# First cross attention of a decoder: weights divided before they are turned, exponentials head by head

## The chip, the cores and the metric

One core of a Trainium2 chip runs the kernel. The metric is device time in microseconds (us) of one execution; the profile is of one execution, taken by the hardware profiler. Engines: PE is TensorE, DVE VectorE, ACT ScalarE, POOL GpSimd, SP SyncE.

## The reference

Two decoder layers, on x of 8 x 256 x 256 and a context of 8 x 120 x 256, f32. Layer 0 is self attention (16 heads of 64), cross attention to the context (16 heads of 16), and a feed-forward stage with rounded weights; layer 1 is a gated attention, a second cross attention and a coupled feed-forward net. A layer norm follows each. What the change touches is the first cross attention:

```
q = split_heads(query @ Wq.T + bq)
k = split_heads(key @ Wk.T + bk)
v = split_heads(value @ Wv.T + bv)
scores = jnp.einsum('bhnd,bhmd->bhnm', q, k)
attn = jax.nn.softmax(scores, axis=-1)
out = jnp.einsum('bhnm,bhmd->bhnd', attn, v)
out = out.transpose(0, 2, 1, 3).reshape(B, N, D_MODEL)
return out @ Wo.T + bo
```

## The kernel before

**Passes.** Four passes (NI), each over two batches (NB), 512 rows in tiles of 128 (T = 4, TS = 2 per batch). one_pass(it, last, then) runs attn0, cross0, ffn0, attn1, cross1 and coupled_ffn. Each engine has its program written out by hand, in an order that never changes, and waits on semaphores (a Signal counts per pass). To fill TensorE, projections of the next pass stand in the stages of this one: values0(then, n), queries0 and keys0. In the last pass `then` is None and spin(n) issues dummy matmuls in some places.

**cross0, a unit.** The work of the first cross attention is cut into UX = 8 units n, in the order batch b = n // 4, half c of the 16 heads = n // 2 % 2, row tile st = n % 2. A unit has HC = 8 heads against M = 120 context columns: 960 score columns on 128 rows. M is 120, S (rows of a batch) 256, P 128, DH 16.

**TensorE.** turn_normed turns the normed x1 of a batch; queries_x(b) projects it; scores_x(n) (matmuls at L757) writes 2 x 480 columns into the pair of banks SCORE_X[n % 2]; turn_x(n) (L770, 16 transposes) turns ex into banks 4 and 5, [120, 1024]; weigh_x(m) (L789), m for batch and half of the heads, takes two units: the first kind of matmuls multiplies by the values vxp, the second by pair_ones and so makes each head's sum, beside it in the same bank; out_x(b) (L525) projects with Wo. scores_x(n) waits until unit n - 2 has been subtracted (dx_done), turn_x(n) for the exponential (px_done) and for the copy of unit n - 1.

**VectorE.** max_x(n): a maximum per row and head (L1954), and, behind a wait for it and for the turning of unit n - 2, the subtraction into ex (L1959), which has two buffers. divide_x(m): a reciprocal of the sums (L1968) and a product into oxt (L1970). sum_2(b) adds the residual (L1928) and calls norm_summed (statistics, L1748 to L1761; GpSimd's power at L2344; apply_norm, L1767). quantize(b) prepares the feed-forward stage, whose first product on VectorE is L1991.

```
for n in range(UX):
    max_x(n)
    if n in (4, 6):
        divide_x(n // 2 - 2)
divide_x(2)
sum_2(0)
divide_x(3)
apply_norm(it, "2", of(res), xs["2"], 0)
quantize(0)
sum_2(1)
```

**ScalarE.** keep (L1341), keep_queries (L1352) and keep_v0 (L1358) copy projections out of PSUM; exp_x(n) is one exponential of 128x960 in place (L1440); keep_tx(n) copies the turned unit into ext (L1446); load_table (L1399) changes the function table.

**GpSimd.** mask_x(m) (L2370) spreads the keys of a half over eight masked copies, kxm, which scores_x(2m) needs; the reciprocal square roots (L2344) stand behind. Elsewhere in its program: scaling of the self attention's weights (L2358), residual plus bias (L2381), a norm with two scalars (L2393).

The self attention of layer 0 already has the form that the change gives to cross0 (exp0 with bias and accumulator at L1388, inverse0 at L1828, L2358 on GpSimd), and so has the exponential of the second cross attention in part (L1614, with bias and accumulator from PSUM, 120x256).

## Time and profile before

| | |
|---|---|
| median of 3 runs | 1120.45 us (1120.40 to 1120.66) |
| profiled execution, its own time | 1121.52 us |
| span of the profiled execution | 1119.8 us |
| mean granted TensorE clock | 0.994 of full speed |
| TensorE, VectorE, ScalarE, GpSimd busy | 92%, 71%, 57%, 28% |
| instructions | 19639 |

The span runs from the first to the last instruction; the execution's own time has what lies around it, 1.7 us. Times in rows are from the start of the span. The second pass's cross0 begins near 377 us and ends near 420, the last pass's near 910 and 950. A busy TensorE is not TensorE at its peak, since ends of matmuls are modelled. "idle before" is the time that an engine waited in front of a row, with what ended the wait.

### The profile page before, as it was taken

What the parts mean: (1) busy time and instruction counts of PE and PEld (TensorE: products, weight loads), DVE (VectorE), ACT (ScalarE), POOL (GpSimd) and SP (SyncE); (2) the same over time, 40 slices, a digit from 0 to 9 for tenths busy, and PEclk for the clock granted to TensorE, in tenths of its full rate; (3) what the DMA queues carried; (4) which work ended last, traced back from release to release, by engine and by line L of the source; (5) the groups of instructions that cost most, each with busy time, mean ns of one, the idle gap of its engine ahead of it and who ended that gap; (6) DMA issues with size and microseconds to landing.
All of it is one profiled execution on the core that took longest, in us unless ns stands there. A gap on an engine that the chain in (4) does not pass through costs nothing.

```text
span 1119.8 us, 19639 instructions
## 1 busy us (share of the span) xinstructions
PE 1031.2 (92%) x7176; PEld 676.7 (60%) x7184; DVE 798.6 (71%) x1880; ACT 635.3 (57%) x1728; POOL 310.3 (28%) x666
## 2 busy tenths in 40 slices
PE   8999999998899999999889999999889998898886
PEld 4477557854557655775547755775455665576463
DVE  3584886668697488658778588666869758864777
ACT  2573556376477257459468365647647724644833
POOL 1264202240056301142108420224004630224110
PEclk9999999999999999999999999999999999999999
DMA  9250000000010000000000000000000000000000
GB/s 345 60 173 1 20 3 7 1 1 1 1 39 1 20 2 9 1 1 1 1 19 21 1 20 1 11 1 1 1 1 20 2 1 1 1 1 1 2 1 20
DMA packets 15951, 22.77 MB, mean 20 GB/s; under 512 B 2160, under 2 KB 13424, under 8 KB 15728
## 3 DMA queue, kind: packets, MB, share of 16 engines
q1 hardware_dynamic: 15408, 21.50, 5.9%
q8 instruction: 58, 0.95, 0.4%
q14 instruction: 37, 0.30, 0.1%
q10 hardware_dynamic: 448, 0.02, 0.0%
HBM read 19.42 MB, written 2.10 MB: 19 GB/s over the span
## 4 chain that ended last, share of the span: by engine, by line
PE 51%; DVE 26%; ACT 12%; issue 6%; POOL 2%; DMA 2%; SPq 0%; DVEq 0%; POOLq 0%; ACTq 0%
PE PS L525 8%; PE PS L929 4%; PE PS L694 4%; ACT work L1388 4%; PE PS L680 3%; PE PS L643 3%; ACT work L1614 3%; PE PS L556 3%; PE PS L898 2%; DVE stat L1748 2%; PE PS L660 2%; PE PS L789 2%; DVE maxx L1954 2%; PE PS L500 2%; DVE work L1959 2%
## 5 line engine op out<-in xcount | busy, mean ns | idle before, releaser
L2344 POOL TENSOR_TENSOR rstd<-var,minus_half 128x2 f32<-128x2 f32 x64 | 45.8, 715 | 529.5 <-DVE var L1761 529.5
L1614 ACT ACTIVATE work<-PS,nmax 120x256 f32<-120x256 f32 x256 | 118.3, 485 | 18.4 <-DVE nmax L2185 17.8
L2185 DVE TENSOR_REDUCE nmax<-PS 120x2 f32<-120x512 f32 x128 | 82.4, 686 | 35.9 <-PE PS L929 35.5
L1821 DVE TENSOR_REDUCE nmax<-PS 128x2 f32<-128x512 f32 x128 | 82.3, 679 | 13.0 <-PE PS L643 13.0
L1388 ACT ACTIVATE work<-PS,nmax 128x256 f32<-128x256 f32 x176 | 81.5, 486 | 15.1 <-DVE nmax L1821 14.9
L2358 POOL TENSOR_SCALAR work<-work,inv 128x256 f32<-128x256 f32 x176 | 81.1, 479 | 0.0
L2339 POOL TENSOR_TENSOR pool_pause<-minus_half 128x1 f32<-128x1 f32 x96 | 28.5, 297 | 182.4 <-DVE inv L1828 94.0
L643 PE MATMUL PS<-work 64*128 64x256 f32 x512 | 70.0, 397 | 6.6 <-ACT work L1388 5.6
L1341 ACT COPY turned_a<-PS 128x512 f32<-128x512 f32 x24 | 14.1, 589 | 100.9 <-PE PS L500 100.9
L643 PEld LDWEIGHTS PS<-work 64*128 64x128 f32 x512 | 44.8, 186 | 27.4 <-ACT work L1388 14.6
L694 PE MATMUL PS<-wo,work 128*128 128x256 f32 x256 | 58.5, 384 | 0.0
L1767 DVE TENSOR_SCALAR x_room<-res,mv,rstd 128x256 f32<-128x256 f32 x96 | 36.0, 416 | 30.2 <-POOL rstd L2344 30.2
L1614 ACT ACTIVATION_READ_ACCUMULATOR work<-PS,nmax 120x1 f32 x256 | 55.6, 217 | 0.0
L694 PEld LDWEIGHTS PS<-wo,work 128*128 128x128 f32 x256 | 47.6, 190 | 8.1 <-issue 1.5
L573 PE MATMUL PS<-turned_x,wk 128*128 128x512 f32 x96 | 50.4, 622 | 0.0
L1440 ACT ACTIVATE work<-work 128x960 f32<-128x960 f32 x32 | 32.1, 1003 | 31.3 <-DVE work L1959 31.3
L1748 DVE BATCH_NORM_STATS2 stat<-res 128x6 f32<-128x256 f32 x128 | 48.1, 418 | 2.0
L556 PE MATMUL PS<-turned_x,wq 128*128 128x512 f32 x96 | 46.4, 596 | 0.0
L525 PE MATMUL PS<-late,turned_a 128*128 128x256 f32 x192 | 46.3, 387 | 0.0
L544 PE MATMUL PS<-wv,turned_x 128*128 128x512 f32 x96 | 46.1, 602 | 0.0
L1954 DVE TENSOR_REDUCE maxx<-PS 128x8 f32<-128x960 f32 x32 | 36.8, 1149 | 12.4 <-PE PS L757 12.4
L680 PE MATMUL PS<-work 128*64 128x256 f32 x352 | 44.4, 385 | 0.0
(275 smaller groups left out, 2535.2 us busy)
## 6 DMA issues: line engine op xcount, KB each, us to landing
turned_x<-in_x_turned_dram SPq DMA_DIRECT2D x4, 512.0 KB, 3.6
xa<-in_x_dram SPq DMA_DIRECT2D x4, 512.0 KB, 4.3
out_dram<-x_room SPq DMA_DIRECT2D x4, 512.0 KB, 3.0
rows<-in_rows_dram SPq DMA_DIRECT2D x1, 1536.0 KB, 10.8
late<-in_L_attn_W_dram SPq DMA_DIRECT2D x2, 768.0 KB, 8.1
wv<-in_attn_v_dram SPq DMA_DIRECT2D x2, 512.0 KB, 5.8
wq<-in_attn_q_dram SPq DMA_DIRECT2D x1, 1024.0 KB, 8.9
wk<-in_attn_k_dram SPq DMA_DIRECT2D x1, 1024.0 KB, 10.9
```

What stands on the lines that cost most here:

```text
L525: mm = pe.matmul(bank(n)[:, (t % 2) * width:(t % 2 + 1) * width], lhs[:, k, t * P:(t + 1) * P], weight[:, k, :], start=(k == 0), stop=(k = ...
L556: mm = pe.matmul(bank(7), wq0[:, k, j * P:(j + 1) * P], turned_x[:, k, :], start=(k == 0), stop=(k == KD - 1))
L643: mm = pe.matmul(bank(2 * (u % 2) + hh)[:, st * S:(st + 1) * S], q0[rows, j, b * S + st * P:b * S + (st + 1) * P], k0[rows, j, b, :], star ...
L680: mm = pe.matmul(bank(6)[hh * DH0:(hh + 1) * DH0, b * S:(b + 1) * S], v0[:, TS * b + tt, (2 * j + hh) * DH0:(2 * j + hh + 1) * DH0], e0t[u ...
L694: mm = pe.matmul(bank(t // 2)[:, (t % 2) * D:(t % 2 + 1) * D], o0t[:, j, t * P:(t + 1) * P], wo0[:, j, :], start=(j == 0), stop=(j == J - 1))
L1388: op = act.activation(e0[u % 3][:, st, hh, :], bank(2 * (u % 2) + hh)[:, st * S:(st + 1) * S], ACT.Exp, bias=nmax0[:, u % 2, hh, st:st + 1 ...
L1614: op = act.activation(e1[:, par, r, kv, :], bank(SCORE_1[r])[0:M, kv * S:(kv + 1) * S], ACT.Exp, bias=nmax1[:, par, r, kv:kv + 1], accum_o ...
L1748: op = dve.bn_stats(stat[:, t, :], src(t))
L1821: dve.tensor_reduce(nmax0[:, u % 2, hh, :], bank(2 * (u % 2) + hh).rearrange("p (t s) -> p t s", t=TS), AX.X, ALU.max, negate=True).then_i ...
L1954: dve.tensor_reduce(maxx[:, n % 2, :].rearrange("p (g h) -> p g h", g=2), banks, AX.X, ALU.max).then_inc(mx_done.sem, 1)
L2185: dve.tensor_reduce(nmax1[:, par, r, :], bank(SCORE_1[r])[0:M, :].rearrange("p (v s) -> p v s", v=2), AX.X, ALU.max, negate=True).then_inc ...
L2358: op = pool.tensor_scalar(e0[u % 3][:, st, hh, :], e0[u % 3][:, st, hh, :], inv0[:, u % 2, hh, st:st + 1], 1.0, ALU.mult, ALU.mult)
```

## The change

- The maximum is written negated (nmaxx). exp_x(n) reads the scores in PSUM, head by head: eight exponentials of 128x120, each with its bias and with its sum over the head's columns (sumx). The subtraction goes.
- inverse_x(n) on VectorE takes the reciprocal of the eight sums; divide_x(n) on GpSimd multiplies the whole unit by it, in place, [128, 8, 120] with the reciprocal broadcast along the 120 columns. turn_x(n) now waits for that (nx_done). ex has three buffers.
- weigh_x has the values' matmuls alone; divide_x(m) on VectorE becomes a copy on ScalarE, keep_ox(m). pair_ones goes.
- keep_tx is on VectorE for units 0, 1, 3, 4, 6 and 7, and stays on ScalarE for 2 and 5.
- The orders of TensorE, ScalarE, VectorE and GpSimd in cross0 are written anew: scores run two units ahead of the turnings, queries_x(0) stands before values0(then, 0), the values of the next pass stand elsewhere, out_x(0) stands before the last two turnings, add_2 and norm_summed are apart; spin(2) in the last pass goes.

The diff, with lines of context left out (eight columns of indent too):

```diff
-pair_ones = sb("pair_ones", [P, 2, 2 * DH])
...
-ex = view(work, K + 1024, P, [2, HC, M])
-maxx = sb("maxx", [P, 2, HC])
+ex = [view(work, K + 1024, P, [HC, M]), view(work, K + 1024 + HC * M, P, [HC, M]), view(work, Q, P, [HC, M])]
+nmaxx, sumx, invx = (sb(n, [P, 2, HC]) for n in ("nmaxx", "sumx", "invx"))
...
-invx = view(work, R + 1440, P, [S])
...
-sx_done, mx_done, dx_done, px_done = (signal(n, UX) for n in ("sx_done", "mx_done", "dx_done", "px_done"))
+sx_done, mx_done, px_done, ix_done, nx_done = (
+    signal(n, UX) for n in ("sx_done", "mx_done", "px_done", "ix_done", "nx_done"))
...
-avx_done, ix_done, ox_kept = (signal(n, NB * KD) for n in ("avx_done", "ix_done", "ox_kept"))
+avx_done, ox_kept = (signal(n, NB * KD) for n in ("avx_done", "ox_kept"))
...
-N_CONST = 12
+N_CONST = 10
...
-            pe.wait_ge(dx_done.sem, dx_done.at(it, n - 1))
+            pe.wait_ge(px_done.sem, px_done.at(it, n - 1))
...
     def turn_x(it, n):
-        pe.wait_ge(px_done.sem, px_done.at(it, n + 1))
+        pe.wait_ge(nx_done.sem, nx_done.at(it, n + 1))
...
-                mm = pe.transpose(bank(4 + half)[0:M, h * 64:(h + 1) * 64], ex[rows, n % 2, h, :], ident[rows, rows])
+                mm = pe.transpose(bank(4 + half)[0:M, h * 64:(h + 1) * 64], ex[n % 3][rows, h, :], ident[rows, rows])
...
-            pe.wait_ge(dx_done.sem, dx_done.at(it, UX))
-        for kind in range(2):
-            for par in range(2):
-                for r in range(4):
-                    lhs = (vxp[:, b, 4 * c + r, par:par + 2, :] if kind == 0 else pair_ones[0:M, par, :])
-                    mm = pe.matmul(bank(WEIGH_X[m])[32 * r:32 * r + 32, kind * S:(kind + 1) * S], lhs,
-                                   ext[:, m % 2, 2 * r + par, :], start=(par == 0), stop=(par == 1))
+            pe.wait_ge(px_done.sem, px_done.at(it, UX))
+        for par in range(2):
+            for r in range(4):
+                mm = pe.matmul(bank(WEIGH_X[m])[32 * r:32 * r + 32, 0:S], vxp[:, b, 4 * c + r, par:par + 2, :],
+                               ext[:, m % 2, 2 * r + par, :], start=(par == 0), stop=(par == 1))
...
     def out_x(it, b):
...
-        pe.wait_ge(dx_done.sem, dx_done.at(it, UX - 1))
+        pe.wait_ge(px_done.sem, px_done.at(it, UX - 1))
...
     def cross0(it, then=None):
         turn_normed(it, "x1", xs["1"], 0)
-        if then is not None:
-            values0(then, 0)
         queries_x(it, 0)
         turn_normed(it, "x1", xs["1"], 1)
...
-            values0(then, 1)
+            values0(then, 0)
         scores_x(it, 0)
         scores_x(it, 1)
         queries_x(it, 1)
         scores_x(it, 2)
+        if then is not None:
+            values0(then, 1)
         turn_x(it, 0)
         scores_x(it, 3)
+        scores_x(it, 4)
         turn_x(it, 1)
-        scores_x(it, 4)
+        if then is not None:
+            values0(then, 2)
+        scores_x(it, 5)
         turn_x(it, 2)
+        scores_x(it, 6)
+        turn_x(it, 3)
         weigh_x(it, 0, then)
-        scores_x(it, 5)
-        turn_x(it, 3)
-        if then is not None:
-            values0(then, 2)
-        scores_x(it, 6)
+        scores_x(it, 7)
         turn_x(it, 4)
+        if then is not None:
+            values0(then, 3)
         weigh_x(it, 1)
-        scores_x(it, 7)
         turn_x(it, 5)
-        if then is not None:
-            values0(then, 3)
+        out_x(it, 0)
         turn_x(it, 6)
+        if then is not None:
+            values0(then, 4)
+        turn_x(it, 7)
         weigh_x(it, 2)
-        turn_x(it, 7)
-        out_x(it, 0)
         weigh_x(it, 3)
-        if then is not None:
-            values0(then, 4)
-        else:
-            spin(2)
         out_x(it, 1)
...
             values0(then, 5)
...
     def cross0(it, then=None):
         def exp_x(n):
-            act.wait_ge(dx_done.sem, dx_done.at(it, n + 1))
-            act.activation(ex[:, n % 2, :, :], ex[:, n % 2, :, :], ACT.Exp).then_inc(px_done.sem, 1)
+            act.wait_ge(mx_done.sem, mx_done.at(it, n + 1))
+            if n > 2:
+                act.wait_ge(tx_done.sem, tx_done.at(it, 2 * n - 4))
+            for h in range(HC):
+                op = act.activation(ex[n % 3][:, h, :], bank(SCORE_X[n % 2] + h // 4)[:, h % 4 * M:(h % 4 + 1) * M], ACT.Exp,
+                                    bias=nmaxx[:, n % 2, h:h + 1], accum_out=sumx[:, n % 2, h:h + 1])
+            op.then_inc(px_done.sem, 1)
...
         def keep_tx(n):
...
+        def keep_ox(m):
+            b, c = m // KD, m % KD
+            act.wait_ge(avx_done.sem, avx_done.at(it, m + 1))
+            act.copy(oxt[:, c, b * S:(b + 1) * S], bank(WEIGH_X[m])[:, 0:S]).then_inc(ox_kept.sem, 1)
+
         keep(it, "x1", 0)
+        keep(it, "x1", 1)
+        keep_queries(it, 0, 4, qx, col["L0_xattn_bq"], qx_done, qx_kept)
...
             keep_v0(then, 0)
-        keep_queries(it, 0, 4, qx, col["L0_xattn_bq"], qx_done, qx_kept)
-        keep(it, "x1", 1)
+        exp_x(0)
+        exp_x(1)
+        keep_queries(it, 1, 5, qx, col["L0_xattn_bq"], qx_done, qx_kept)
+        exp_x(2)
...
             keep_v0(then, 1)
-        exp_x(0)
-        keep_queries(it, 1, 5, qx, col["L0_xattn_bq"], qx_done, qx_kept)
-        exp_x(1)
-        keep_tx(0)
-        exp_x(2)
-        keep_tx(1)
         exp_x(3)
+        exp_x(4)
         keep_tx(2)
-        exp_x(4)
-        keep_tx(3)
+        exp_x(5)
...
             keep_v0(then, 2)
-        exp_x(5)
-        keep_tx(4)
+        keep_ox(0)
         exp_x(6)
+        exp_x(7)
+        keep_ox(1)
+        if then is not None:
+            keep_v0(then, 3)
         keep_tx(5)
-        exp_x(7)
-        keep_tx(6)
-        if then is not None:
-            keep_v0(then, 3)
-        keep_tx(7)
+        keep_ox(2)
+        keep_ox(3)
...
             keep_v0(then, 4)
...
         apply_norm(it, "1", of(res), xs["1"], 1)
...
-        def sum_2(b):
+        def add_2(b):
...
-            norm_summed(it, "2", b)
...
         def max_x(n):
...
-            dve.tensor_reduce(maxx[:, n % 2, :].rearrange("p (g h) -> p g h", g=2), banks, AX.X, ALU.max
+            dve.tensor_reduce(nmaxx[:, n % 2, :].rearrange("p (g h) -> p g h", g=2), banks, AX.X, ALU.max, negate=True
...
-            dve.wait_ge(mx_done.sem, mx_done.at(it, n + 1))
+
+        def inverse_x(n):
+            dve.wait_ge(px_done.sem, px_done.at(it, n + 1))
...
-                dve.wait_ge(tx_done.sem, tx_done.at(it, 2 * n - 2))
-            dve.tensor_tensor(ex[:, n % 2, :, :].rearrange("p (g h) m -> p g h m", g=2), banks,
-                              maxx[:, n % 2, :].rearrange("p (g h o) -> p g h o", g=2, o=1).to_broadcast([P, 2, 4, M]),
-                              ALU.subtract).then_inc(dx_done.sem, 1)
-
-        def divide_x(m):
-            b, c = m // KD, m % KD
-            dve.wait_ge(avx_done.sem, avx_done.at(it, m + 1))
-            if m > 0:
-                dve.wait_ge(ox_kept.sem, ox_kept.at(it, m))
-            dve.reciprocal(invx[:, :], bank(WEIGH_X[m])[:, S:2 * S]).then_inc(ix_done.sem, 1)
-            dve.wait_ge(ix_done.sem, ix_done.at(it, m + 1))
-            dve.tensor_tensor(oxt[:, c, b * S:(b + 1) * S], bank(WEIGH_X[m])[:, 0:S], invx[:, :], ALU.mult
-                              ).then_inc(ox_kept.sem, 1)
-
-        for n in range(UX):
-            max_x(n)
-            if n in (4, 6):
-                divide_x(n // 2 - 2)
-        divide_x(2)
-        sum_2(0)
-        divide_x(3)
+                dve.wait_ge(nx_done.sem, nx_done.at(it, n - 1))
+            dve.reciprocal(invx[:, n % 2, :], sumx[:, n % 2, :]).then_inc(ix_done.sem, 1)
+
+        def keep_tx(n):
+            dve.wait_ge(tx_done.sem, tx_done.at(it, 2 * n + 2))
+            if n > 3:
+                dve.wait_ge(avx_done.sem, avx_done.at(it, n // 2 - 1))
+            dve.tensor_copy(ext[:, n // 2 % 2, :, n % 2 * P:(n % 2 + 1) * P].rearrange("p h (f i) -> p f h i", f=2),
+                            PS[0:M, 4:6, :].rearrange("p f (h i) -> p f h i", i=64)).then_inc(tx_kept.sem, 1)
+
+        max_x(0)
+        max_x(1)
+        inverse_x(0)
+        max_x(2)
+        inverse_x(1)
+        keep_tx(0)
+        max_x(3)
+        inverse_x(2)
+        max_x(4)
+        keep_tx(1)
+        inverse_x(3)
+        max_x(5)
+        inverse_x(4)
+        max_x(6)
+        keep_tx(3)
+        inverse_x(5)
+        max_x(7)
+        inverse_x(6)
+        keep_tx(4)
+        inverse_x(7)
+        add_2(0)
+        keep_tx(6)
+        norm_summed(it, "2", 0)
+        keep_tx(7)
         apply_norm(it, "2", of(res), xs["2"], 0)
         quantize(0)
-        sum_2(1)
+        add_2(1)
+        norm_summed(it, "2", 1)
         apply_norm(it, "2", of(res), xs["2"], 1)
         quantize(1)
...
+        def divide_x(n):
+            pool.wait_ge(ix_done.sem, ix_done.at(it, n + 1))
+            pool.tensor_tensor(ex[n % 3][:, :, :], ex[n % 3][:, :, :],
+                               invx[:, n % 2, :].unsqueeze(2).to_broadcast([P, HC, M]), ALU.mult).then_inc(nx_done.sem, 1)
+
         mask_x(2)
+        divide_x(0)
+        divide_x(1)
         mask_x(3)
+        for n in range(2, UX):
+            divide_x(n)
         rstds_of(it, "2")
...
-    pool.memset(pair_ones[:, :, :], 0.0).then_inc(filled.sem, 1)
-    pool.wait_ge(filled.sem, 7)
-    pool.memset(pair_ones[:, 0, 0:DH], 1.0).then_inc(const_ready.sem, 1)
-    pool.memset(pair_ones[:, 1, DH:2 * DH], 1.0).then_inc(const_ready.sem, 1)
+    pool.wait_ge(filled.sem, 6)
...
-    pool.wait_ge(filled.sem, 9)
+    pool.wait_ge(filled.sem, 8)
...
```

## Rows read from the trace of the kernel before

**Rows 1.** The page: busy time of the engines, and the chain of waits by engine

```profile
PE 1031.2 (92%) x7176; PEld 676.7 (60%) x7184; DVE 798.6 (71%) x1880; ACT 635.3 (57%) x1728; POOL 310.3 (28%) x666
...
PE 51%; DVE 26%; ACT 12%; issue 6%; POOL 2%; DMA 2%; SPq 0%; DVEq 0%; POOLq 0%; ACTq 0%
```

**Rows 2.** Chain of waits, second pass: start us, us, what

```profile
419.45 0.70 DVE res L1928
...
425.44 1.29 DVE work L1991
```

**Rows 3.** Timeline of PE, second pass: start us, us, engine, line, operation [idle before]

```profile
394.29 1.07 PE L789 MATMUL PS<-work,vxp 120*32 120x256 f32 x16
395.18 1.05 PE L789 MATMUL PS<-work,pair_ones 120*32 120x256 f32 x16
...
416.38 1.99 PE L525 MATMUL PS<-x0TWo,work 128*128 128x256 f32 x8 [0.43 <-DVE work L1970]
```

**Rows 4.** Timeline of DVE, second pass

```profile
384.72 1.16 DVE L1954 TENSOR_REDUCE maxx<-PS 128x8 f32<-128x960 f32 x1 [3.54 <-PE PS L757]
385.91 1.16 DVE L1959 TENSOR_TENSOR work<-PS,maxx 128x960 f32<-128x960 f32 x1
...
403.02 1.76 DVE L1968 RECIPROCAL work<-PS 128x256 f32<-128x256 f32 x1
404.81 0.42 DVE L1970 TENSOR_TENSOR work<-PS,work 128x256 f32<-128x256 f32 x1
```

**Rows 5.** Groups by form on DVE, whole span: busy us, mean ns, idle before

```profile
L1828 DVE RECIPROCAL inv<-sum 128x4 f32<-128x4 f32 x64 | 11.2, 175 | 19.3 <-ACT work L1388 15.5 <-ACT x_room L1388 1.9
```

**Rows 6.** Timeline of ACT, second pass

```profile
388.01 0.82 ACT L1352 ACTIVATE work<-PS,cols 128x256 f32<-128x256 f32 x2
389.36 1.00 ACT L1440 ACTIVATE work<-work 128x960 f32<-128x960 f32 x1 [0.53 <-DVE work L1959]
390.27 0.99 ACT L1446 COPY work<-PS 120x1024 f32<-120x1024 f32 x1
```

**Rows 7.** Timeline of ACT in the second cross attention, first pass

```profile
258.26 0.47 ACT L1614 ACTIVATE work<-PS,nmax 120x256 f32<-120x256 f32 x1
258.63 0.19 ACT L1614 ACTIVATION_READ_ACCUMULATOR work<-PS,nmax 120x1 f32 x1
...
259.62 0.48 ACT L1614 ACTIVATE work<-PS,nmax 120x256 f32<-120x256 f32 x1
```

**Rows 8.** Groups by form on ACT, whole span

```profile
L1589 ACT ACTIVATE xh_room<-PS,cols 128x256 f32<-128x256 f32 x48 | 20.1, 470 | 19.2 <-PE PS L898 19.2
...
L1673 ACT ACTIVATE work<-PS,g_b 64x128 f32<-64x128 f32 x8 | 2.8, 356 | 5.8 <-PE PS L1006 5.8
```

**Rows 9.** Groups by form on POOL, whole span

```profile
L2358 POOL TENSOR_SCALAR work<-work,inv 128x256 f32<-128x256 f32 x176 | 81.1, 479 | 0.0
...
L2393 POOL TENSOR_SCALAR x_room<-res,mv,rstd_h 128x256 f32<-128x256 f32 x16 | 20.5, 1284 | 0.9
L2381 POOL TENSOR_TENSOR x_room<-x_room,rows 128x1024 f32<-128x1024 f32 x4 | 9.4, 2352 | 3.4 <-DVE x_room L1767 3.4
```

**Rows 10.** Stretches: length, busy us by engine, then granted PE clock, DMA, GB/s

```profile
383.60:418.30 34.70, 31.39 (x326) 17.50 (x326) 30.24 (x39) 20.02 (x24) 3.82 (x12) 1.00 0.03 10
418.30:445.87 27.57, 26.92 (x143) 15.26 (x143) 23.75 (x62) 19.26 (x25) 2.53 (x3) 1.00 0.03 10
...
264.00:268.00 4.00, 2.67 (x32) 1.41 (x32) 3.59 (x9) 3.81 (x13) 0.00 (x0) 1.00 0.00 0
```

**Rows 11.** The same for two stretches of the last pass

```profile
934.00:936.00 2.00, 0.43 (x13) 0.32 (x10) 1.97 (x3) 1.73 (x2) 0.00 (x0) 0.96 0.00 0
936.00:938.00 2.00, 2.00 (x28) 1.37 (x32) 1.97 (x2) 0.00 (x0) 0.00 (x0) 0.50 0.00 0
```

**Rows 12.** Timeline of DVE, last pass

```profile
915.50 1.16 DVE L1954 TENSOR_REDUCE maxx<-PS 128x8 f32<-128x960 f32 x1 [1.76 <-PE PS L757]
...
950.14 0.68 DVE L1928 TENSOR_TENSOR res<-PS,x_room 128x512 f32<-128x512 f32 x1
```

More of the change, by code:

```diff
@@ L1152, in cross0 @@
                 scores_x(it, 2)
+                if then is not None:
+                    values0(then, 1)
                 turn_x(it, 0)
                 scores_x(it, 3)
+                scores_x(it, 4)
                 turn_x(it, 1)
-                scores_x(it, 4)
-                turn_x(it, 2)
-                weigh_x(it, 0, then)
-                scores_x(it, 5)
-                turn_x(it, 3)
                 if then is not None:
                     values0(then, 2)
+                scores_x(it, 5)
+                turn_x(it, 2)
                 scores_x(it, 6)
+                turn_x(it, 3)
+                weigh_x(it, 0, then)
+                scores_x(it, 7)
                 turn_x(it, 4)
-                weigh_x(it, 1)
-                scores_x(it, 7)
-                turn_x(it, 5)
                 if then is not None:
                     values0(then, 3)
+                weigh_x(it, 1)
+                turn_x(it, 5)
+                out_x(it, 0)
                 turn_x(it, 6)
-                weigh_x(it, 2)
-                turn_x(it, 7)
-                out_x(it, 0)
-                weigh_x(it, 3)
                 if then is not None:
                     values0(then, 4)
-                else:
-                    spin(2)
+                turn_x(it, 7)
+                weigh_x(it, 2)
+                weigh_x(it, 3)
                 out_x(it, 1)
```

2 lines of the change are left out of this document (1 added, 1 removed).

## The prediction

> **What bounds the kernel now.** I read four views in this order. The page [rows 1] says that TensorE is busy 92% of the span and carries half of the chain of waits, VectorE a quarter. That is an average; the change touches one stage, so the rest is read there. The stage runs once in each of the four passes; the second pass (turning of x1 from about 377.5 us) stands for the first three, the last pass has no work of a next pass in it.
>
> The chain of waits [rows 2] runs over VectorE at the stage's end: the sum of the second batch at 419.45, then with no other engine but one short GpSimd step the first gate product at 425.44. The timelines say why. VectorE works almost without a gap from 384.72: a maximum (1.15) and a subtraction (1.16) for each of eight units, and four times a reciprocal (1.76) and a product (0.42) [rows 4]. ScalarE is slack: one exponential of 960 columns takes 1.00 [rows 6], and from 383.60 to 418.30 it is busy 20.02 us of 34.70. TensorE is busy 31.39 us of that stretch, and behind the stage, from 418.30 to 445.87, it is busy 26.92 of 27.57 [rows 10]. So behind the stage TensorE and VectorE run nearly level: what makes out_x(1) late makes everything late, with 0.65 us of TensorE's gaps as the only cushion.
>
> **The change part by part.** *VectorE* loses eight subtractions (9.3 us) and four reciprocals with products (8.7 us) and gains six copies of turned weights (960 columns take 1.16 [rows 4], so 1024 some 1.22 and six 7.3 us) and eight small reciprocals (175 ns each [rows 5]). It becomes slack until exp_x(7). *TensorE* loses the row sums: in each of four weigh_x the pair_ones half, of the length of the first half, which starts 0.89 before it (394.29, 395.18 [rows 3]); with the hand-over 3.7 us per pass. The score, turn and projection matmuls stay. *Set-up* loses three memsets of GpSimd at the very start, while TensorE waits for its first weights: nothing. The two dummy matmuls of the last pass go as well: no cost by themselves. No transfer is added, removed or moved.
>
> *GpSimd* gets one product of 128x960 per unit. The trace does not show it. Nearest is the in-place product-shaped TENSOR_TENSOR of 128x1024 with a broadcast operand, 2.35 us, so 2.2; the dearest form per column is L2393, 1284 ns for 256, which would make 4.8; the cheapest, the scaling by a scalar (479 for 256), 1.8 [rows 9]. I take 2.2, as the operation is the same and the size nearly so; that its broadcast runs along the inner index, and not the outer, no row prices. Queued behind these products on GpSimd is mask_x(3), which scores_x(6) needs five microseconds later: hidden. Who waits for the product is turn_x, with everything behind it in TensorE's fixed order.
>
> *ScalarE* is where the bill comes. An exponential of 960 columns starts the next instruction 0.91 after its own start (389.36 to 390.27 [rows 6]). It becomes eight of 120 columns, each with an accumulator read. The heads' price: L1614, an exponential from PSUM with bias and accumulator, starts every 0.453 us at 256 columns (258.26 to 259.62 is three) [rows 7]. An activation of 128 columns is 114 ns shorter than one of 256, 356 against 470 [rows 8], 0.89 ns per column; a plain pair of 256 (0.82 for two, less the 0.09 that an instruction overlaps the next, so 0.37 each) against the 0.91 for 960 gives 0.77 [rows 6]. For 136 columns fewer that is 0.105 to 0.121. A head costs **0.337**, a unit 2.70 instead of 0.91. Bounds: 0.45 if nothing is saved with width; 0.26 if the read (0.08, from 0.453 against the plain 0.37) were free. 0.337 is a reading between rows that differ only in width, so I hold 0.325 to 0.35 for near certain unless the read behaves otherwise.
>
> The Trainium skill ("ScalarE: Activation LUTs", section "What ACT_TABLE_LOAD costs") gives an ACTIVATE with a pointer bias about 280 ns + 0.833 per column, less 93 of overlap; an estimate by it alone is 0.287 a head, and the sum below would come to between -1 and -2 us instead of +10. It prices no accumulator read; at 256 columns it gives 0.400, and this trace shows 0.453.
>
> Now the walk, second pass. The first maximum ends at 385.88 as before [rows 4] (the values that moved behind the queries fill the same time). From there ScalarE's queue never waits: each scores_x(n) waits for exp_x(n-2), and 0.1 + 0.9 (matmuls) + 1.15 (maximum) = 2.2 us fit under the 2.70 of exp_x(n-1), as does inverse 0.2 + product 2.2 + turning 0.6 = 3.0 under two exponentials, the three buffers allowing that. In the queue stand eight units, 21.6, keep_queries(1) 0.75, two value copies 1.0, one keep_tx 0.92, one keep_ox 0.35: 24.6 us. exp_x(7) ends at **410.5**. Behind it: keep_ox(1) 0.35, hand-over 0.15, out_x(0) 1.9 (413.0), turning 6 0.6, values 1.9 (415.5), turning 7 0.6 (416.1). VectorE meanwhile does add_2(0) 0.7, keep_tx(6) 1.2, the statistics 1.3 (416.2), only then keep_tx(7), which sits in front of the last weighing: 417.4. Then weigh 3 1.0, keep_ox(3) 0.4, hand-overs 0.3, out_x(1) 1.9: it ends at **420.9**, against 418.3 (416.38 and 1.9 [rows 3]): +2.6 us. The 3.7 us that TensorE is spared become gaps, since it waits for exponentials and then for keep_tx(7) and keep_ox(3).
>
> VectorE's side: the second sum starts at 421.0 instead of 419.45 [rows 2], +1.5. TensorE's side: its work up to the end of the feed-forward stage is unchanged, with 0.65 us of gaps [rows 10], which a shift can use up in part: +2.6 less 0.3 = +2.3. The larger one counts: **+2.3** in each of the first three passes. Nothing later in a pass gives it back, because both engines are full up to 445.87.
>
> The last pass: the copy of queries_x(0) now stands behind the copy of the second turning on ScalarE, and scores_x(0) waits for it with no values as cover, so the first maximum starts 1.5 us later than at 915.50 [rows 12] and the first exponential at 918.1. The queue is 1.0 shorter without the value copies, but waits 0.5 in sum for maxima: exp_x(7) ends at 942.2, and with the same tail of 10.4 out_x(1) ends at 952.6. The second sum, at 950.14 before [rows 12], starts at 952.7: **+2.5**. There the granted clock stands at 0.50 from 936 to 938, its lower level of 1.2 GHz, behind 2 us with TensorE 0.43 us busy [rows 11]. With TensorE waiting for exponentials about half the time this comes again, likely more than once, and the tail has 6 us of TensorE work in the chain; a slice of 2 us at half rate adds 1. I add **+1**.
>
> Sum: 3 x 2.3 + 2.5 + 1 = +10.4. The profiled execution took 1121.52 for a span of 1119.8; the median of the runs is 1120.45, 0.1% less. Against the median the change gives 1130.9, rounded **1130.5**. A run can tell about 0.2% (2.2 us) from no change.
>
> **Rivals.**
> 1. *The accumulator read half hides behind the next head.* A head then costs 0.30, midway between 0.337 and the lower bound of 0.26. Every 0.01 us is 64 heads x 0.01 = 0.64 a pass, so 0.037 less takes the 2.3 a pass to 0: 1120 to 1122, within 0.2%. For it: the read's record overlaps its neighbours. Against: the start distance of 0.453 has that overlap in it already [rows 7]. 12%. The estimate of 0.287 by the Trainium skill ("ScalarE: Activation LUTs") lies on this side of the forecast; by it the time would be about 1119.
> 2. *The other side: faster.* The same place, ScalarE's queue of 64 heads; it decides at 0.30 a head, below which the 18 us of VectorE and 3.7 us of TensorE begin to pay. With the read wholly free, 0.26, the queue is 4.9 us shorter than forecast; TensorE's order then binds and passes on some 4.3 of it, -2.0 a pass: 1113. 14%.
> 3. *GpSimd becomes the bound*: above 3.1 us a product the eight in a row outlast the exponentials, at 3.4 the pass gains 4.5 (1139), at 4.8 16 us (1184). For it: the L2393 form; against: the 1024 product [rows 9]. 7%.
> 4. *The clock falls in the first three passes too.* Around 391.6 to 395.0 TensorE would be busy some 45%. One slice at half rate per pass costs about 1.3: 1134 to 1137. Against: 264 to 268 has TensorE busy 2.67 of 4 us and keeps 1.00 [rows 10]. 12%.
> The forecast itself, head 0.325 to 0.35 and no more: 55%, 1126 to 1134.
>
> **How the numbers follow.** The point is the forecast's. The range from 1118.5 to 1137 holds the forecast, rivals 1 and 4; it leaves out rival 3 and the fast part of rival 2, together under 0.2. Slower: 0.55 + 0.07 + 0.12 = 0.74; within 0.2%: 0.12; faster 0.14.
>
> **What would show it.** Right: 256 activations of 128x120 (eight heads, eight units, four passes), starting every 0.34; ScalarE without a gap from the first maximum to the eighth unit, the eighth ending 24.6 us after the first starts; maxima waiting for scores; the product on GpSimd near 2.2; TensorE's idle before keep_tx and keep_ox; the second sum 1.5 us later within the pass. Wrong: a head under 0.30 or over 0.37, a GpSimd product over 3.1, ScalarE waiting for maxima, or a slow clock in the middle passes.

## The result, and where the time went

The changed kernel takes **1137.38 us** (median of 4 runs, 1135.72 to 1145.51), the kernel before beside it 1120.49: a ratio of 1.0162, with an interval of 1.0142 to 1.0183. That is +16.9 us where I had forecast +10, and 0.4 us above my range. Two more measurements of the same kernel (both in experiment 2) gave ratios of 1.0119 and 1.0136.

The profiled execution took 1136.96 us for a span of 1134.5, 14.7 more than the span of before. The page of the kernel after, its busy times and its chain by engine, against [rows 1]:

```profile
PE 1024.7 (90%) x6916; PEld 673.3 (59%) x6924; DVE 763.1 (67%) x1872; ACT 673.7 (59%) x2200; POOL 368.7 (32%) x695
...
PE 51%; ACT 19%; DVE 19%; issue 6%; POOL 3%; DMA 2%; SPq 0%; DVEq 0%; POOLq 0%; ACTq 0%
...
L1438 ACT ACTIVATE work<-PS,nmaxx 128x120 f32<-128x120 f32 x256 | 89.9, 471 | 9.2 <-DVE nmaxx L1956 9.2
...
L2402 POOL TENSOR_TENSOR work<-work,invx 128x960 f32<-128x960 f32 x32 | 57.3, 1791 | 37.0 <-DVE invx L1963 37.0
```

VectorE's busy time fell by 35 us and ScalarE's share of the chain rose from 12% to 19%. (The 471 ns of an exponential is the length of its record, which overlaps its neighbours; the start distance is what counts.) GpSimd's product takes 1.79 us.

Where in the program the time goes is read by setting the same event of both traces side by side. I take two: VectorE's first sum of a pass (ahead of the first cross attention) and its second output sum (behind it). Timeline of VectorE of the kernel before, second and last pass:

```profile
373.42 0.69 DVE L1916 TENSOR_TENSOR res<-PS,xa 128x512 f32<-128x512 f32 x1 [6.47 <-PE PS L694]
...
905.97 0.69 DVE L1916 TENSOR_TENSOR res<-PS,xa 128x512 f32<-128x512 f32 x1 [6.47 <-PE PS L694]
```

The second sums of before stand in [rows 2] (419.45) and [rows 12] (950.14). The same of the kernel after:

```profile
374.62 0.69 DVE L1919 TENSOR_TENSOR res<-PS,xa 128x512 f32<-128x512 f32 x1 [6.47 <-PE PS L693]
...
422.50 0.69 DVE L1931 TENSOR_TENSOR res<-PS,x_room 128x512 f32<-128x512 f32 x1 [0.44 <-PE PS L524]
...
912.49 0.69 DVE L1919 TENSOR_TENSOR res<-PS,xa 128x512 f32<-128x512 f32 x1 [6.47 <-PE PS L693]
...
966.30 0.69 DVE L1931 TENSOR_TENSOR res<-PS,x_room 128x512 f32<-128x512 f32 x1 [3.41 <-PE PS L524]
```

I call the distance from the one to the other **the stage**. Before it is 46.03 us in the second pass (and in the first and third) and 44.17 in the last; after it is 47.88 (+1.85) and **53.81 (+9.64)**. Some 23 us later the feed-forward stage adds 0.37 in each of the first three passes, which makes 2.22 a pass. Between the stages the two traces drift apart or together by up to 1.6 us (+0.54 ahead of the first stage, -1.57 from the first pass to the second, +0.76 to the last, -1.43 behind it). Three of these four go with short stretches at a granted clock near 0.7, at 285 to 295 us and at 1055 to 1060 before, and at 810 to 815 after. Every trace of this study has such stretches outside the last stage, at changing places, and I treat what they cost as noise.

So three passes behave alike and the last does not. Timeline of TensorE in the last pass of the kernel after, and its windows (length, busy us of PE, PEld, DVE, ACT, POOL, granted clock, DMA share, GB/s):

```profile
922.38 3.55 PE L756 MATMUL PS<-work 64*128 64x480 f32 x8 [1.42 <-ACT work L1347]
...
951.05 3.78 PE L524 MATMUL PS<-x0TWo,work 128*128 128x256 f32 x8 [0.60 <-ACT work L1452]
954.76 1.11 PE L769 MATMUL PS<-ident,work 64*120 64x64 f32 x16
957.31 1.11 PE L769 MATMUL PS<-ident,work 64*120 64x64 f32 x16 [1.44 <-DVE work L1969]
958.35 3.64 PE L786 MATMUL PS<-work,vxp 120*32 120x256 f32 x32
962.48 3.78 PE L524 MATMUL PS<-x0TWo,work 128*128 128x256 f32 x8 [0.49 <-ACT work L1452]
```

```profile
383.60:418.30 34.70, 28.05 (x243) 14.43 (x241) 18.72 (x29) 28.15 (x141) 19.37 (x20) 1.00 0.05 17
...
946.00:950.00 4.00, 2.19 (x47) 1.49 (x45) 2.46 (x3) 4.00 (x27) 2.77 (x2) 0.96 0.00 0
950.00:954.00 4.00, 3.40 (x16) 2.67 (x13) 0.20 (x1) 1.91 (x7) 1.88 (x2) 0.50 0.00 0
954.00:958.00 4.00, 2.56 (x31) 1.74 (x32) 2.71 (x7) 0.00 (x0) 0.00 (x0) 0.50 0.00 0
958.00:962.00 4.00, 3.99 (x40) 1.55 (x37) 3.68 (x13) 0.37 (x1) 0.71 (x1) 0.50 0.02 4
962.00:966.00 4.00, 3.52 (x8) 2.86 (x9) 0.85 (x3) 1.86 (x3) 0.00 (x0) 0.50 0.00 0
```

Both out_x take 3.78 us where [rows 3] has 1.99: from 950 to 966 TensorE is granted 0.50, its level of 1.2 GHz, and in this stretch the chain of waits runs over TensorE (from 951.05 to 966.28 it names another engine for 1.6 us alone). The clock was low earlier in this stage too, for shorter stretches: the scores of units 0 and 1 take 3.55 us at 922.38, where two in a row take 1.88 in the second pass. In the second pass (first row) the same stage keeps 1.00.

### The profile page after: what moved, and what is told of

Its sections match the earlier page's. It is cut to its first block, busy times and chain, and to the rows that moved or that the text cites. A ratio compares the mean times of both kernels' runs of the same rounds, so it can differ in the third digit from the quotient of the medians.

```text
span 1134.5 us, 19620 instructions
## 1 busy us (share of the span) xinstructions
PE 1024.7 (90%) x6916; PEld 673.3 (59%) x6924; DVE 763.1 (67%) x1872; ACT 673.7 (59%) x2200; POOL 368.7 (32%) x695
## 4 chain that ended last, share of the span: by engine, by line
PE 51%; ACT 19%; DVE 19%; issue 6%; POOL 3%; DMA 2%; SPq 0%; DVEq 0%; POOLq 0%; ACTq 0%
PE PS L524 9%; ACT work L1438 7%; PE PS L926 4%; ACT work L1383 3%; PE PS L679 3%; PE PS L642 3%; PE PS L693 3%; PE PS L555 3%; PE PS L895 2%; ACT work L1617 2%; PE PS L543 2%; DVE stat L1751 2%; PE PS L659 2%; POOL rstd L2361 2%; PE PS L499 2%
## 5 line engine op out<-in xcount | busy, mean ns | idle before, releaser
L1438 ACT ACTIVATE work<-PS,nmaxx 128x120 f32<-128x120 f32 x256 | 89.9, 471 | 9.2 <-DVE nmaxx L1956 9.2
L1438 ACT ACTIVATION_READ_ACCUMULATOR work<-PS,nmaxx 128x1 f32 x256 | 74.9, 317 | 0.0
L2402 POOL TENSOR_TENSOR work<-work,invx 128x960 f32<-128x960 f32 x32 | 57.3, 1791 | 37.0 <-DVE invx L1963 37.0
L642 PEld LDWEIGHTS PS<-work 64*128 64x128 f32 x512 | 44.7, 186 | 27.5 <-ACT work L1383 14.7
L1956 DVE TENSOR_REDUCE nmaxx<-PS 128x8 f32<-128x960 f32 x32 | 36.7, 1156 | 34.6 <-PE PS L756 34.6
L756 PE MATMUL PS<-work 64*128 64x480 f32 x128 | 36.4, 653 | 21.2 <-ACT work L1438 19.8
## 6 DMA issues: line engine op xcount, KB each, us to landing
rows<-in_rows_dram SPq DMA_DIRECT2D x1, 1536.0 KB, 10.8
```

The lines of the kernel that those rows point to most:

```text
L642: mm = pe.matmul(bank(2 * (u % 2) + hh)[:, st * S:(st + 1) * S], q0[rows, j, b * S + st * P:b * S + (st + 1) * P], k0[rows, j, b, :], star ...
L1438: op = act.activation(ex[n % 3][:, h, :], bank(SCORE_X[n % 2] + h // 4)[:, h % 4 * M:(h % 4 + 1) * M], ACT.Exp, bias=nmaxx[:, n % 2, h:h + ...
```

## The experiments

My theory after the result: **ScalarE's queue costs 2.2 to 2.5 us a pass as forecast, and TensorE's half clock in the last pass costs 7 more.** Rivals: the two dropped dummy matmuls did it; GpSimd's product did it; the loss comes with the gaps and not with the clock; the place of the low clock is chance.

**1. The dropped dummies alone, and dummies in all gaps.** a0_spin2 puts back what the change dropped:

```diff
                 weigh_x(it, 3)
+                if then is None:
+                    spin(2)
                 out_x(it, 1)
```

a1_spins has such lines at thirteen places, 56 dummies in the last pass (its text on record says 61, that of a5_light_spins 60; both are miscounts), three of which the changed kernel has as well, behind out_x(1): behind the second turning 5, queries 1: 3, scores 2: 9, scores 3: 4, turn_x 1: 6, and so on. b1_before_spins gives the kernel before six, ahead of turn_x(5).

> The changed kernel with the two dummy matmuls put back before the last out_x of the last pass, which the change dropped with its else branch. Main theory (TensorE runs at 1.2 GHz in the last pass because its short instructions lie apart for some 25 us in that stretch, long before these dummies): two dummies behind the last weigh_x come too late, so the last pass keeps its loss of 9.7 us and the time stays within 1 us of the changed kernel, about 1137. Rival (the dropped dummies alone let the clock fall): the last pass loses 2.5 us instead of 9.7, about 1130.

> The changed kernel with 61 dummy matmuls in the gaps of TensorE in the last pass's cross0, beside the same work. Main theory (7.2 us of the last pass's loss of 9.7 are TensorE at half clock, 2.5 us are the queue of ScalarE as in the other passes): the granted clock stays 1.00 from 910 to 970 us, the two last weigh_x and out_x take 1.99 us or less instead of 3.6 to 3.8, and the time falls by 6 to 8 us, to about 1130. Rival (the low clock only follows from a stretch that waits for ScalarE, and costs little by itself): the clock is back, the time falls by 2 us or less, to 1135 or more.

> The kernel before with six dummy matmuls ahead of turn_x(5) in the last pass, where its own granted clock stood at 0.66. Main theory: the low clock of the kernel before is short and lies where TensorE waits for others, so it was worth 1 us at most: 1119.5 to 1120.5. Rival: it was worth 2 us or more, so the last pass of the kernel before is no clean reference, and the loss by the clock in the changed kernel is larger than 7.2 us.

Measured (kernel before beside them 1121.02): a0 1135.3, ratio 1.013 [1.0109, 1.015]; its last stage takes 48.87 us in the one trace, at a clock of 0.58 to 0.87 in four of the 5-us windows from 935 to 960, and a further stretch at 0.5 to 0.8 lies at 825 to 840. The stage loses 4.7 us here and not the 9.7 that I expected; the stretch at 825 to 840 lies outside it, and the distance from the third stage to the last is 225.45 us against 221.39 in the kernel after. The low clock stays, so the dropped dummies are not its cause; whether they soften it the runs do not say, since a0's ratio lies between those of the unaltered change. b1 1121.14, ratio 1.0002 [0.9992, 1.0011], stage 44.26: its six dummies lift the clock from 935 to 940 from 0.66 to 1.00, and no time comes back. So the kernel before loses nothing there and is a clean reference.

a1 is a miss: 1140.0, ratio 1.0176. The clock is 1.00 from 905 to 970, but the last stage takes 55.07 us. Timeline of TensorE in a1_spins:

```profile
929.59 4.15 PE L626 MATMUL PS<-upto,ones 128*128 128x256 f32 x18
...
938.55 2.86 PE L626 MATMUL PS<-upto,ones 128*128 128x256 f32 x12
```

Nine dummies take 4.15 us, six take 2.86: one is two instructions and 0.46 to 0.48 us, not the 0.23 I had reckoned with. TensorE was busy 63.6 of the 65 us from 905 to 970, so the filling itself probably became the bound. This kernel tells nothing about the clock's price.

**2. Light dummies, and the change itself again.** a5_light_spins has 27 dummies (2, 2, 5, 2, 3, 2, 2, 3, 1, 2, 1, 1 in the gaps and 1 behind the last out_x, where the changed kernel has 3), some 13 us in all by the figures of a1_spins.

> The changed kernel with 27 dummy matmuls, in the gaps of TensorE in the last pass's cross0 (a1_spins had 60 there, and each took 0.43 us where I had reckoned with 0.23, so that they themselves filled the engine). Main theory (the low clock costs the last pass 7.2 us): granted clock 1.00 from 910 to 970 us, the last pass loses 2.4 us from its first sum to its second instead of 9.66, and the time is 1129 to 1131. Rival (a gap that is filled pushes back as much as the clock gives, however light the filling): 1135 or more.

> The changed kernel itself once more, with a second trace. Main theory (TensorE's half clock in the last pass's cross0 is the kernel's own doing and comes back in each execution): the last pass loses 7 to 10 us in this trace as well, with the granted clock at 0.5 to 0.9 between 915 and 970 us. Rival (the place wanders, and the first trace showed one chance case): the last pass loses under 4 us, the clock falls elsewhere, and the time is the same 1136 to 1138 all the same, or lower.

a5_light_spins: **1131.37**, ratio 1.0101 [1.0083, 1.0119]. after_again, in another session: 1133.61, ratio 1.0119 [1.0104, 1.0134], last stage 50.32 us, 6.15 more than before where I expected 7 to 10, again with the clock at 0.50 from 934 to 942 and from 950 to 960. So the half clock comes back in the last pass, but the two kernels now seemed only 0.2% apart, and the clock's price was open between 2 and 7 us. They had to run on one chip:

> The changed kernel for the third time, beside the one with light dummies on one chip, since its first two measurements differ (1.0162 and 1.0119 of the kernel before). Theory A (the half clock in the last pass is always there, but how much of TensorE's critical work falls into it varies from execution to execution): granted clock below 0.99 of the span again, last pass 50 to 54 us from first sum to second, time 1133 to 1138. Theory B (the first measurement was that chip's own): 1131.5 or less.

> The changed kernel with the 27 light dummies in the last pass, as a5_light_spins. Theory A: last pass 47.1 us, time 1130 to 1131.5, and 3 to 6 us under pair_after on the same chip: that difference is what the clock costs. Theory B: within 1.5 us of pair_after.

pair_after **1136.70** (5 runs, 1131.38 to 1138.37; ratio 1.0136 [1.0112, 1.016]), pair_light_spins **1129.66** (1129.15 to 1131.22; ratio 1.008 [1.0066, 1.0094]): 7.0 us between the medians, where I had expected 3 to 6. The first and the second sum of the last pass, VectorE's timeline of pair_after:

```profile
912.23 0.69 DVE L1919 TENSOR_TENSOR res<-PS,xa 128x512 f32<-128x512 f32 x1 [6.47 <-PE PS L693]
...
966.01 0.69 DVE L1931 TENSOR_TENSOR res<-PS,x_room 128x512 f32<-128x512 f32 x1 [3.41 <-PE PS L524]
```

and of pair_light_spins, with its windows of TensorE (length, busy, granted clock, DMA share, GB/s) and its last out_x in a third fence:

```profile
914.21 0.69 DVE L1943 TENSOR_TENSOR res<-PS,xa 128x512 f32<-128x512 f32 x1 [6.47 <-PE PS L693]
...
961.26 0.69 DVE L1955 TENSOR_TENSOR res<-PS,x_room 128x512 f32<-128x512 f32 x1 [0.51 <-PE PS L524]
```

```profile
950.00:954.00 4.00, 3.80 (x43) 1.00 0.00 0
954.00:958.00 4.00, 3.62 (x46) 1.00 0.02 4
958.00:962.00 4.00, 3.87 (x32) 1.00 0.00 0
```

```profile
959.22 1.99 PE L524 MATMUL PS<-x0TWo,work 128*128 128x256 f32 x8
```

The stage takes 53.78 us in the one and 47.05 in the other, 6.7 less. The two traced executions as a whole differ by 4.7 us only (1135.93 and 1131.22): pair_light_spins has stretches of low clock at 270 to 280 and 555 to 565 us, outside the stage, and its distance from the second stage to the third is 1.6 us longer. That settles the sign: work was added to TensorE on one chip, and it brought the clock to 1.00 and time back; out_x takes 1.99 us there instead of 3.78. The size is less fixed. What is left of the last pass's loss is 47.05 - 44.17 = 2.9 us, so the clock's part is 6.7 in the traces of the kernel after and of pair_after and 50.32 - 47.05 = 3.3 in that of after_again. Single runs of the changed kernel go the same way (1131.38 us at a mean clock of 0.990, 1138.37 at 0.985), which fits the unequal ratios.

**3. What ScalarE's queue costs.** a3_no_sums is a1_spins without the accumulator; the sums are left out, and the reciprocal is taken of a constant:

```diff
-    bias=nmaxx[:, n % 2, h:h + 1], accum_out=sumx[:, n % 2, h:h + 1])
+    bias=nmaxx[:, n % 2, h:h + 1])
```

> The kernel with the dummy matmuls (a1_spins), and the sums of the exponentials left out: the 256 activations have no accumulator and the reciprocal is taken of a constant. A head then has one instruction. Main theory (ScalarE's queue from the first maximum to exp_x(7) sets the pass; an accumulator read makes a head 0.337 us instead of about 0.26): the 64 heads of a pass are 4.9 us shorter and nearly all of it comes back, 4 us a pass and 16 in all, to about 1114. Rival (TensorE's written order, or GpSimd's chain of products, is close behind the queue of ScalarE): 2 us a pass or less, 1122 or more.

1125.05, 15.0 less than a1_spins. ScalarE's timeline: sixteen heads with nothing between them, in a3_no_sums,

```profile
382.89 4.12 ACT L1462 ACTIVATE work<-PS,nmaxx 128x120 f32<-128x120 f32 x16 [1.62 <-DVE nmaxx L1980]
386.79 0.95 ACT L1371 ACTIVATE work<-PS,cols 128x256 f32<-128x256 f32 x2
```

so a head is (386.79 - 382.89) / 16 = 0.244 us, and the accumulator's read costs 0.337 - 0.244 = 0.093. The stage of the second pass falls from 47.81 to 42.98: of 64 x 0.093 = 6.0 us, 4.8 come back. The first three passes give 14.5 of the 15.0; the last stage gives 0.3 (55.07 to 54.79), with the same 53 dummies in front of the last out_x in both. So in the first three passes ScalarE's queue is the bound. The absolute forecast of 1114 rested on a1 being at 1130 and missed for that reason; the amount per pass is the theory's. The Trainium skill ("ScalarE: Activation LUTs", section "What ACT_TABLE_LOAD costs") gives about 280 ns + 0.833 per column, less 93 of overlap, for an activation with a pointer bias and prices no read; the estimate from that is 0.287 for 120 columns. This case's trace does not agree: the measured 0.244 lies below it, and the 0.337 with the read above it.

**4. GpSimd's product.** a4_half_product is a5_light_spins with the product over heads 0 to 3 alone (half of the division is left out).

> a5_light_spins with GpSimd's product over the first four heads of each unit alone (half of the division is left out). Main theory (the product of 1.79 us is hidden behind the 2.70 us that ScalarE takes for a unit, but stands once at the end of the chain, behind exp_x(7)): a product of 0.9 us takes at most 0.9 us off a pass, so 1 to 3.5 us in all. Rival (GpSimd bounds the units): about 0.9 us on each of the last units, 3 us a pass or more, over 10 us in all.

1130.04 against 1131.37. The product takes 0.99 us instead of 1.79, and the stage of the second pass stays at 47.88 (a5_light_spins: 47.87), the last at 47.05 (47.05). So GpSimd's product is hidden altogether in the stage; even the 0.9 us that I allowed at the end of the chain is not there: in the kernel after, the reciprocal of unit 7 starts at 412.13 and the product is done some 2 us later, while TensorE comes to turn_x(7) at 416.87. The 1.3 us between the two kernels fall into the range that I expected, but not for my reason: they lie outside the stages, where the traces drift anyway.

**5. The move of the division alone.** u0_whole_units divides ahead of the turning like the change, but takes the exponentials whole. TensorE, ScalarE and VectorE have new orders for that:

```diff
-    for h in range(HC):
-        op = act.activation(ex[n % 3][:, h, :], ...
+    act.activation(ex[n % 3][:, :, :], ex[n % 3][:, :, :], ACT.Exp).then_inc(px_done.sem, 1)
...
+    dve.tensor_tensor(ex[n % 3][:, :, :].rearrange("p (g h) m -> p g h m", g=2), banks, ...
+    dve.tensor_reduce(sumx[:, n % 2, :], ex[n % 3][:, :, :], AX.X, ALU.add)
```

> The weights still divided ahead of their turning, by reciprocals, on GpSimd, but no unit goes head by head: VectorE subtracts the maximum of the whole unit, ScalarE takes one wide exponential, VectorE sums the unit; orders walked for that, 23 dummy matmuls in the last pass. This is the division's move alone, without the accumulated exponentials. Main theory (the move of the division as such costs nothing, the accumulated exponentials on ScalarE do): walked, 1.1 us less than the kernel before in each of three passes and 0.5 more in the last, 1118; with the 0.9 us a pass by which the two reordered kernels ran behind their walk, 1121. Rival (the longer chain of a unit, maximum to turned weight by way of GpSimd, costs in any case): 1125 or more.

1123.48, ratio 1.0028 [1.0017, 1.0038] (26 dummies, not 23). Its stage takes 46.46 us in the second pass, +0.43, and 44.40 in the last, +0.23. So the division can stand in front for next to nothing, where the whole change costs 1.85 and 2.9: that the longer chain of a unit costs in any case is refuted. How the rest splits between the heads and the orders this run does not show, since both differ from the change; h1_reordered, below, has the heads in other orders and a shorter stage still. The time is 2.5 us above the 1121 that I expected.

**6. Other orders.** h1_reordered keeps every operation of the change and moves copies from ScalarE to VectorE, with other orders on TensorE and 23 dummies in the last pass. In short form, the values' copies left out:

```diff
-ScalarE:  ... exp_x(4) keep_tx(2) exp_x(5) keep_ox(0) exp_x(6) exp_x(7) keep_ox(1) keep_tx(5) ...
+ScalarE:  ... exp_x(4) exp_x(5) exp_x(6) exp_x(7) load_table keep_tx(6) keep_tx(7) keep_ox(2) keep_ox(3)
+VectorE:  keep_tx(0) to (5), keep_ox(0) and (1) between maxima and reciprocals
+TensorE:  scores_x(0) ahead of the second turning; values0 at other places
```

w1_mixed_units also takes units 0, 2, 4 and 6 whole, as in u0, and only 1, 3, 5 and 7 head by head.

> The changed kernel's operations in other queue orders (values0 and weigh_x moved on TensorE; turned weights kept by VectorE for units 0 to 5 and by ScalarE for 6 and 7, where the changed kernel has ScalarE keep 2 and 5 in between the exponentials; the first two outputs kept by VectorE; exp_x(0) ahead of nothing it need not wait for), with 23 dummy matmuls in the last pass. Main theory (the loss is the work in ScalarE's queue between the first maximum and exp_x(7), and can be taken out of it): walked with the measured durations, a pass ends 3.2 us earlier than in the kernel before, 5.4 earlier than in the changed one, so about 1107 to 1109. Rival (these orders already wait for one another in a circle, so that moving the copies only moves the wait): no more than 1 us a pass, 1126 or more.

> As h1_reordered, but units 0, 2, 4 and 6 take the way of the kernel before for their exponentials (VectorE subtracts the maximum of the whole unit, ScalarE takes one wide exponential of 0.98 us, VectorE sums it), and only the odd units go head by head; orders walked for that mix, 16 dummy matmuls in the last pass. Main theory (ScalarE and VectorE are to share a unit's work: ScalarE loses 4 times 1.7 us, VectorE gains 4 times 2.3): a pass ends 3.8 us earlier than in the kernel before and the last 5, so about 1104 to 1106. Rival (VectorE, which has some 40 us of cross0, becomes the bound, or every hand-over between the two costs more than walked): 1110 or more.

h1 1117.89, ratio 0.9973 [0.9961, 0.9984]: stage 44.26 in the second pass (-1.77 to before, -3.6 to the change), half of the walked gain to before, and 43.13 in the last (-1.04). The trace is of the fastest of nine runs (1113.12 us; seven took 1116.53 to 1118.89), so the stages say 6.4 us where the medians say 2.5, and no trace shows where the slower runs lose the rest. w1 (18 dummies, not 16) **1110.74**, ratio 0.9918 [0.9899, 0.9936]: stage 43.49 (-2.54) and 41.00 in the last (-3.17). Both ran behind the walk, w1 in the range of its rival, but both beat the kernel before.

Where h1 gains is not where I looked for it. Second pass of the kernel after, keep_ox(1) and out_x(0), then of h1_reordered the first and the last of the 64 heads and out_x(0):

```profile
411.70 0.66 ACT L1452 COPY work<-PS 128x256 f32<-128x256 f32 x1
412.41 1.99 PE L524 MATMUL PS<-x0TWo,work 128*128 128x256 f32 x8 [0.89 <-ACT work L1452]
```

```profile
381.84 0.36 ACT L1460 ACTIVATE work<-PS,nmaxx 128x120 f32<-128x120 f32 x1
...
406.24 0.55 ACT L1460 ACTIVATE work<-PS,nmaxx 128x120 f32<-128x120 f32 x1
```

```profile
405.59 1.99 PE L524 MATMUL PS<-x0TWo,work 128*128 128x256 f32 x8
```

From its first head to the end of its last the queue takes 24.7 us in h1 as in the kernel after (24.6). It starts 11.3 us behind the stage's first sum (370.56 in h1) instead of 12.4, and what follows the last head, up to the second sum (414.82), takes 8.2 us instead of 10.8: out_x(0) starts before the last head, since the copy that it waits for, keep_ox(1), stands on VectorE and no longer behind exp_x(7). So the queue of the heads did not get shorter; less of the pass stands behind it.

**7. The best version, with and without dummies.**

> w1_mixed_units without its 16 dummy matmuls in the last pass. Main theory (in the last pass, which has no values0 to fill TensorE, the engine's gaps let the granted clock fall, and the slower matmuls then stand on the path): the last pass from its first sum to its second loses 2 to 7 us against w1_mixed_units's 41.0, and the time is 1113 to 1118. Rival (the shorter cross0 leaves gaps too short for the clock to fall, so dummies are not needed there): 1111 or less.

> w1_mixed_units once more, beside the changed kernel on one chip, for the ratio of the two. Main theory: 1110 to 1112, 2.3% under the changed kernel and 0.8% under the kernel before. Rival (the first result lay on a fast chip): 0.5% under the kernel before or less.

> w0_no_spins once more, on the same chip: 1109 to 1111, 0.8 to 1.0% under the kernel before and 2 to 2.4% under the changed one. It would be wrong if it came out above 1114.

w0_no_spins 1109.70, ratio 0.9912 [0.9895, 0.9928], beside w1_again 1111.75, 0.9923 [0.9908, 0.9938]; pair_mixed 1109.45, 0.9899 [0.9885, 0.9912]. Here my clock theory missed in its reach: without dummies the last stage takes 40.47 us, less than with them (41.00), although the clock falls from 918 to 926. Windows of TensorE in w0_no_spins (length, busy, granted clock, DMA share, GB/s):

```profile
918.00:922.00 4.00, 2.12 (x22) 0.84 0.00 0
922.00:926.00 4.00, 3.53 (x38) 0.73 0.01 4
926.00:930.00 4.00, 3.36 (x53) 1.00 0.00 0
930.00:934.00 4.00, 3.77 (x54) 1.00 0.00 0
```

The clock is back at 1.00 before the tail; of the chain one scores_x at 921.65 takes 1.95 us instead of 1.07. So a low clock in the last pass does not cost by itself, it costs where the chain runs over TensorE. pair_mixed ran beside pair_after: 1109.45 against 1136.70.

## Why the prediction was right in three passes and wrong in the fourth

- **The head, 0.337 us: right.** ScalarE's timeline in the kernel after, the rows between the exponentials being the accumulator's:

```profile
387.06 0.36 ACT L1438 ACTIVATE work<-PS,nmaxx 128x120 f32<-128x120 f32 x1 [1.62 <-DVE nmaxx L1956]
387.32 0.19 ACT L1438 ACTIVATION_READ_ACCUMULATOR work<-PS,nmaxx 128x1 f32 x1
...
389.77 0.40 ACT L1438 ACTIVATE work<-PS,nmaxx 128x120 f32<-128x120 f32 x1
```

(389.77 - 387.06) / 8 = 0.339. Rivals 1 and 2 needed 0.30 or less.
- **The queue of 24.6 us: right.** keep_ox(1) starts behind the last head at 411.70, 24.64 after 387.06; less the 1.20 by which this pass begins later than before, exp_x(7) ends at 410.5, as walked.
- **The tail: right.** The last out_x of the pass:

```profile
418.90 1.07 PE L786 MATMUL PS<-work,vxp 120*32 120x256 f32 x16 [0.35 <-DVE work L1969]
420.47 1.99 PE L524 MATMUL PS<-x0TWo,work 128*128 128x256 f32 x8 [0.49 <-ACT work L1452]
```

  By the same 1.20 it starts at 419.27, where the walk had 419.0. The weighing waits for keep_tx(7) and out_x for keep_ox(3), the two I named. The pass loses 2.22 us against 2.3. That the two lie so near is in part luck: with its 1.99 us out_x(1) ends 2.9 us later than before, not 2.6, and the feed-forward stage takes up 0.7 of it, not 0.3.
- **The product on GpSimd: 1.79, not 2.2**, under the rival of 3.1 and hidden. The row that it lay nearest to was the cheap bound, the scaling by a scalar [rows 9].
- **The last pass without the clock: +2.5, measured +2.9** (pair_light_spins). There the first head starts 12.2 us behind the first sum and exp_x(7) ends 36.7 behind it; the walk had 12.1 and 36.2.
- **The step that failed is "I add +1" for the granted clock in the last pass.** It measured 6.7 us in the traces of the kernel after and of pair_after, and 3.3 in that of after_again. I had priced one slice of 2 us, the length seen in the kernel before [rows 11], though I wrote that the low clock would come likely more than once. With ScalarE as the bound TensorE has a gap in front of nearly every step, and in the kernel after the clock falls several times. The last fall (950 to 966) covers the tail: both out_x and the last two weigh_x take 3.78, 3.78 and 3.64 us instead of twice 1.99 and twice 1.07, which alone is 5.1 us. From the start of out_x(0) to the second sum the kernel after takes 15.25 us and pair_light_spins 9.90, so 5.35 of the 6.7 are lost in the tail, and 1.4 ahead of it, where the scores at 922.38 are. I had written "6 us of TensorE work in the chain" in the same sentence; at half clock that makes +6 for the tail instead of +1, a sum of +15.4 or 1135.9, 1.5 under the result.
- **Rival 4 was placed wrongly.** The slow clock in the first three passes did not come: from 383.60 to 418.30 it is 1.00, with TensorE busy 28.05 of 34.70 us. That values0 is what keeps it up there no run isolates; the dummies that do so in the last pass speak for it.

Without the clock term my sum was +9.4, 1129.9; the kernel with light dummies takes 1129.66 and, measured the first time, 1131.37. The Trainium skill ("TensorE: Matmul & The Clock Gate", section "A second HAM failure mode: psum-queue depth-cycling") says of a kernel that cycles through PSUM banks that frequent small idle times between its groups of matmuls make the clock swing between its levels. The last pass agrees (0.50 from 950 to 966); the second pass, with its gaps of about 1 us in front of each scores_x, does not.

## What to carry to other kernels

Splitting one wide activation into heads to save VectorE a pass over the data pays for itself only while ScalarE is slack: 64 small ones with accumulators took 21.6 us where eight wide ones had taken 7.3. What the next engine needs early should then not stand behind the last of them. All heads in other orders came out 0.3% under the kernel before, and sharing the units between both forms (every second one whole) 0.8 to 1.0%. When an edit makes TensorE wait, price the half clock by all the TensorE work in the chain behind the gaps, not by the slice seen so far, and take that as an upper bound: here it cost 3.3 to 6.7 us, and in w0_no_spins nothing that shows in the time. Test it with a few dummies in the stretch that nothing else fills, after measuring how long one dummy takes.

## What was not expected of the hardware

- Adding work made the kernel faster: 27 dummies where the changed kernel has 3, each some 0.5 us, took 7.0 us off the median (1136.70 to 1129.66), in a kernel in which TensorE was not the bound by its busy time.
- The read of an accumulator costs the next head 0.093 us (0.337 less 0.244), though its record, 0.19 to 0.49 us in the kernel after, lies over the neighbouring records.
- GpSimd's product of 128x960 with one value per head takes 1.79 us, 1.86 ns per column, where the product-shaped operation of 128x1024 with a broadcast row takes 2.35 [rows 9], 2.30 ns per column; over half the columns, 480, it takes 0.99. The one multiplies and the other adds, so these rows do not say whether the operation or the form of the broadcast makes the difference.
